# A decoder layer's attention loop: queries transposed when only centred, and a new order of the work within a step

## The chip, the cores and the metric

One core of a Trainium2 chip runs the whole layer in one launch. The metric is the device time of a run in microseconds (us). Three runs of the kernel before took 506.27, 509.51 and 511.21 us; the median is 509.51 us. The profile is one more execution, with its own time.

## The reference

x is 64 sequences of 64 tokens with 128 features; ctx_1024 has the same shape. All is float32.

```
p    = layernorm(x) @ Wv.T + bv                      # self-attention, q = k = v = p, 16 heads of 8
x    = x + softmax(p p' / sqrt(8)) p @ Wo.T + bo
q    = layernorm(x)                                  # cross-attention, no projection
x    = x + softmax(q ctx' / sqrt(8)) ctx
h    = layernorm(x)                                  # shared SwiGLU expert and one of 7 routed experts
x    = x + 0.5 / tw * shared(h) + switched(h) / tw
layernorm(x) = (x - mean) / sqrt(var + 1e-5)
```

## The kernel before, in words

**Units and steps.** A unit is 128 tokens, that is two sequences; there are 32. The first phase (`phase_a`, line 181) carries every unit through both attentions and up to the router's product. It is a software pipeline: in step t, of 38 in all, each letter of the table `DELAY` (line 177) works on the unit t minus its delay: n (first layer norm) 0, p (projections) 1, s (self-attention) 2, o (its output leaves) 3, x (residual, second layer norm, cross scores) 4, y (the weighing of cross-attention) 5, r (third layer norm, router) 6. So up to seven units are in work at once. Phases for the shared expert and the routed experts follow, from about 330 us on; the change does not touch them.

**What sets the order.** Each engine has a function `body(t, u, live)` that is written out for all steps; an engine works off its instructions strictly in the order in which `body` lists them, and waits at each for counts of semaphores. Nothing is planned at run time. A wait therefore holds up everything behind it on its engine.

**One step, by engine.** The tensor engine (PE, line 460) does: the self scores of s (L426), the transposition of the normalised tokens of p (L468), of the cross probabilities of y (L435, eight matmul records), the projections (L476, L481), the weighing of y (L447), the transposition of the normalised cross queries of x (L492), the cross scores (L426), the transposition of the self probabilities (L435), the turning back of y's output (L457), the transposition of r's tokens (L506), of o's attention output (L511), the weighing of s (L447), the router's product (L518), the output projection of o (L523), and the turning back of s (L457). Its next step begins with the self scores again. ScalarE (ACT, line 640) copies transposed tiles out of PSUM and takes the exponentials (L613); late in a step it does `exp("x", .., 0)`, then the eviction `oT_s` (L626), then `exp("x", .., 1)`. VectorE (DVE, line 797) does moments (`moments`, `mean_variance`), the residual sum (L807), the maxima of each score row and their subtraction (L769, L776) and the reciprocals and products that normalise the outputs (L784, L792). GpSimd (POOL, line 329) turns mean and variance into normalised tiles: four small instructions for the second layer norm (L334 to L342), the same for the first and third together, then the bias sum (L366), the masked keys `k_s` (L371) and y's residual sum (L376). In the code `xn["s"]` is the normalised tile of the second norm, `ps_oT`, `ps_wo` and `ps_qT` are one and the same quarter of a PSUM bank.

**The way through memory.** The self-attention output `on_s` of o is written to DRAM by head and read back by token (`orow`). The sync engine's queue (SP, line 259) issues it: two writes, four loads of cross keys, then after the writes have landed the read of `orow`, two loads of cross values, four more of keys, and a prefill. The read of `orow` is issued and waited for in the same step (L511).

These lines order the projection before:

```
if live("o"):                                         # PE, end of step t, unit t - 3
    pe.wait_ge(sem("s_onT"), at(u["o"]))
    nc.tensor.matmul(ps_wo, onT[:], wo_sb[:], start=True, stop=True).then_inc(sem("s_wo"), 1)
if live("x"):                                         # DVE, start of step t + 1, the same unit
    dve.wait_ge(sem("s_wo"), at(u["x"]))
```

Of the kernel before, what the change touches and what calls it, by code (L numbers as in the profile page):

```python
# [27 lines left out]
DK = D // H  # L28
# [29 lines left out]
def build(nc, x, ctxk, ctxv, wv, bv, wo, bo, rw, rb, wup, wdn, ident, hmask, tri, small, tokens, out):  # L58
    ctx = ExitStack()
    with ctx:  # L60
# [242 lines left out]
        def _(pool):  # L303
# [25 lines left out]
            def body(t, u, live):  # L329
                i = t % 2  # L330
                pool.wait_ge(sem("mv_set"), 2)
                if live("x"):
                    pool.wait_ge(sem("s_mv"), at(u["x"]))
                    nc.gpsimd.tensor_scalar(ve[:, 0:1], mv[i][:, 0:1, 1], EPS, None, ALU.add).then_inc(sem("s_ve"), 1)  # L334
                    if u["x"] >= 2:
                        pool.wait_ge(sem("s_xn"), u["x"] - 1)
                    pool.wait_ge(sem("s_ve"), at(u["x"]))
                    nc.gpsimd.tensor_tensor(rs[i][:, 0:1], ve[:, 0:1], mhalf[:, 0:1], ALU.pow).then_inc(sem("s_rs"), 1)
                    nc.gpsimd.tensor_scalar(nmean[i][:, 0:1], mv[i][:, 0:1, 0], -1.0, None, ALU.mult).then_inc(sem("s_mean"), 1)
                    pool.wait_ge(sem("s_rs"), at(u["x"]))  # L340
                    pool.wait_ge(sem("s_mean"), at(u["x"]))
                    normed("s", t, u["x"], xn["s"][:], "s_qT")  # L342
# [19 lines left out]
                if live("o"):  # L362
                    if u["o"] == 0:
                        pool.wait_ge(sem("obias"), 1)
                    pool.wait_ge(sem("p_xn"), at(u["o"]))
                    nc.gpsimd.tensor_tensor(x_all[:, u["o"], :], x_all[:, u["o"], :], obias[:], ALU.add).then_inc(sem("p_xb"), 1)  # L366
                if live("p"):
# [49 lines left out]
        def _(pe):  # L417
# [42 lines left out]
            def body(t, u, live):  # L460
                if live("s"):
                    pe.wait_ge(sem("s_khd"), at(u["s"]))
                    scores("s", u["s"], pT, k_s)
                if live("p"):
# [4 lines left out]
                if live("y"):  # L469
                    turn("x", u["y"], 0)  # L470
                    turn("x", u["y"], 1)
                if live("p"):
# [34 lines left out]
                if live("o"):  # L507
                    pe.wait_ge(sem(f"w_rows{u['o'] % 2}"), 16 * (u["o"] // 2 + 1))
                    if u["o"] >= 1:
                        pe.wait_ge(sem("x_q"), u["o"])  # L510
                    nc.tensor.transpose(ps_oT, orow[u["o"] % 2][:], id_sb[:]).then_inc(sem("s_oT"), 1)  # L511
# [7 lines left out]
                if live("o"):  # L519
                    if u["o"] == 0:  # L520
                        pe.wait_ge(sem("obias"), 1)
                    pe.wait_ge(sem("s_onT"), at(u["o"]))
                    nc.tensor.matmul(ps_wo, onT[:], wo_sb[:], start=True, stop=True).then_inc(sem("s_wo"), 1)  # L523
# [81 lines left out]
        def _(act):  # L605
# [5 lines left out]
            def exp(k, u, g):  # L611
# [28 lines left out]
            def body(t, u, live):  # L640
                weights_of_step(t)
                if live("p"):
# [8 lines left out]
                if live("s"):  # L651
                    exp("s", u["s"], 0)
                if live("x"):
                    act.wait_ge(sem("s_qT"), at(u["x"]))
                    if u["x"] >= 1:
                        act.wait_ge(sem("x_sc"), u["x"])
                    nc.scalar.copy(qT[:], ps_qT).then_inc(sem("x_q"), 1)  # L657
# [7 lines left out]
                if live("s"):  # L665
                    exp("s", u["s"], 1)
# [16 lines left out]
                if live("o"):  # L683
                    act.wait_ge(sem("s_oT"), at(u["o"]))
                    if u["o"] >= 1:
                        act.wait_ge(sem("s_wo"), u["o"])
                    nc.scalar.copy(onT[:], ps_oT).then_inc(sem("s_onT"), 1)
                if live("x"):
                    exp("x", u["x"], 0)
                if live("s"):  # L690
                    evicted("s", u["s"])
                if live("x"):
                    exp("x", u["x"], 1)
# [42 lines left out]
        def _(dve):  # L736
# [15 lines left out]
            def mean_variance(k, t, u):  # L752
                dve.wait_ge(sem(f"{k}_st"), at(u))
                dve.wait_ge(sem("mv_set"), 2)
                if k == "s" and u >= 2:
                    dve.wait_ge(sem("s_ve"), u - 1)
                    dve.wait_ge(sem("s_mean"), u - 1)
# [3 lines left out]
                nc.vector.bn_aggr(mv[t % 2][:, NORM[k], :], st[k][:]).then_inc(sem(f"{k}_mv"), 1)  # L761

# [34 lines left out]
            def body(t, u, live):  # L797
                if live("n"):
                    if u["n"] in X_LOADS:
                        dve.wait_ge(sem(X_LOADS[u["n"]]), 16)  # L800
                    moments("p", u["n"])
                if live("n"):
                    mean_variance("p", t, u["n"])
                if live("x"):
# [3 lines left out]
                if live("o"):  # L808
                    invert("s", u["o"])
                if live("x"):  # L810
# [221 lines left out]
```

## Time and profile before

| | |
|---|---|
| median of three runs | 509.51 us (506.27 to 511.21) |
| profiled execution | 505.83 us, its span 503.8 us |
| PE busy | 426.8 us, 85% of the span |
| PE weight loads | 321.6 us, 64% |
| DVE busy | 324.7 us, 64% |
| ACT busy | 280.8 us, 56% |
| POOL busy | 288.5 us, 57% |
| mean granted PE clock | 0.956 of full speed |

The span runs from the first to the last instruction; some 2 us of the execution lie around it. Busy shares are means over phases with different limits. PE's matmuls are pipelined, and the ends in the trace are modelled, so the distance from the start of one block to the start of the next says more than a duration. "L160" is the line of the helper that issues nearly all DMAs. Idle time named "issue" is idle with nothing in the profile to wait for.

### The profile page before, as it was taken

The page shows a single profiled execution, that of the slowest core. Times are in us where ns is not written, and L with a number is a line of the kernel's source. Part 1 is how long each engine was busy: PE and PEld are TensorE (multiplying, and loading weights), DVE is VectorE, ACT ScalarE, POOL GpSimd, SP SyncE. Part 2 cuts the span into 40 slices and gives each one's busy share as a digit, 9 for nine tenths or more (in the row PEclk, how much of TensorE's full clock was granted, in tenths as well). Part 3 has the DMA queues.
Part 4 walks back from the last instruction along what each step waited for, and adds up shares of the span by engine and source line. Part 5 has one row for each costly group of instructions (what it writes and reads, how often), then busy time and mean ns, then how long its engine had stood idle before and what let it go on. Part 6 is the DMA issues. An engine that isn't in the chain of part 4 may idle for free. (4 is left out here: it accounts for less than half of the span.)

```text
span 503.8 us, 16733 instructions
## 1 busy us (share of the span) xinstructions
PE 426.8 (85%) x5528; PEld 321.6 (64%) x5529; DVE 324.7 (64%) x959; ACT 280.8 (56%) x695; POOL 288.5 (57%) x493
## 2 busy tenths in 40 slices
PE   1688799888898988999898987588999759999991
PEld 0345456555555655555555555378999759999990
DVE  5547688875876878787887875366555514444441
ACT  2237677675676776777767664322222226666660
POOL 6867577675576676767767663404544503444443
PEclk9999999997998999999999997779999959999997
DMA  4223533544444545533332333001112134540000
GB/s 107 57 36 46 94 54 47 92 83 77 81 70 69 110 73 88 93 46 52 45 53 40 54 38 69 2 0 54 63 63 73 64 105 128 135 127 27 29 31 6
DMA packets 171647, 32.55 MB, mean 65 GB/s; under 512 B 147507, under 2 KB 169014, under 8 KB 171584
## 3 DMA queue, kind: packets, MB, share of 16 engines
q1 hardware_dynamic: 161696, 19.50, 24.6%
q10 hardware_dynamic: 7136, 5.90, 4.3%
q0 software_dynamic: 2752, 6.33, 3.6%
q8 instruction: 36, 0.59, 0.5%
q14 instruction: 27, 0.22, 0.2%
HBM read 18.26 MB, written 13.83 MB: 64 GB/s over the span
## 5 line engine op out<-in xcount | busy, mean ns | idle before, releaser
L853 DVE TENSOR_TENSOR gT<-gT,bank 128x384 f32<-128x384 f32 x70 | 38.7, 554 | 68.1 <-PE bank L542 58.7
L769 DVE TENSOR_REDUCE mx_x<-bank 128x8 f32<-128x512 f32 x64 | 41.2, 686 | 45.4 <-PE bank L426 45.4
L406 POOL DMA_INDIRECT out<-yrow,token x38 | 37.3, 982 | 55.0 <-DVE yrow L967 43.4
L701 ACT ACTIVATE gT<-bank 128x384 f32<-128x384 f32 x70 | 34.1, 487 | 53.0 <-PE bank L542 51.4
L371 POOL TENSOR_TENSOR k_s<-pT,hmask_sb 128x1024 f32<-128x1024 f32 x32 | 60.9, 1902 | 3.5 <-ACT pT L664 3.5
L551 PE MATMUL bank<-wdn_sb,gT 128*128 (+1 forms) x420 | 58.7, 276 | 2.9 <-DVE rowb L863 2.3
L542 PE MATMUL bank<-fhT,wtile 128*128 128x128 f32 x456 | 59.7, 283 | 0.0
L397 POOL DMA_INDIRECT sorted_rows<-rowb,place x32 | 31.0, 967 | 44.7 <-DVE rowb L863 28.7
L542 PEld LDWEIGHTS bank<-fhT,wtile 128*128 128x128 f32 x456 | 56.4, 199 | 0.3 <-issue 0.3
L551 PEld LDWEIGHTS bank<-wdn_sb,gT 128*128 128x128 f32 x420 | 52.7, 192 | 3.8 <-DVE gT L853 2.7
L542 PE MATMUL bank<-hT_all,wup_sb 128*128 (+1 forms) x384 | 49.4, 280 | 0.0
L769 DVE TENSOR_REDUCE mx_s<-bank 128x8 f32<-128x512 f32 x64 | 43.6, 681 | 5.4 <-PE bank L426 5.4
L542 PEld LDWEIGHTS bank<-hT_all,wup_sb 128*128 128x128 f32 x384 | 46.8, 197 | 0.0
L776 DVE TENSOR_TENSOR pr_s<-bank,mx_s 128x512 f32<-128x512 f32 x64 | 44.3, 692 | 2.2
L435 PEld LDWEIGHTS bank<-id_sb,pr_s 128*128 128x128 f32 x256 | 28.6, 146 | 26.8 <-ACT pr_s L613 26.8
L426 PE MATMUL bank<-ring,qT 64*64 64x512 f32 x256 | 35.2, 619 | 12.2 <-ACT qT L657 9.4
L613 ACT ACTIVATE pr_s<-pr_s 128x512 f32<-128x512 f32 x64 | 40.6, 635 | 3.8 <-DVE pr_s L776 3.7
L613 ACT ACTIVATE pr_x<-pr_x 128x512 f32<-128x512 f32 x64 | 40.5, 635 | 1.3 <-DVE pr_x L776 1.2
L647 ACT COPY xnT<-bank 128x128 f32<-128x128 f32 x32 | 8.5, 265 | 58.4 <-PE bank L468 58.4
L776 DVE TENSOR_TENSOR pr_x<-bank,mx_x 128x512 f32<-128x512 f32 x64 | 40.9, 681 | 0.0
L620 ACT COPY prT_s<-bank 128x512 f32<-128x512 f32 x64 | 34.6, 589 | 10.1 <-PE bank L435 10.0
L620 ACT COPY prT_x<-bank 128x512 f32<-128x512 f32 x64 | 34.8, 589 | 9.2 <-PE bank L435 9.0
(136 smaller groups left out, 917.1 us busy)
## 6 DMA issues: line engine op xcount, KB each, us to landing
sorted_rows<-nowhere_row SPq DMA_DIRECT2D x38, 129.0 KB, 2.9
ring<-sorted_rows SPq DMA_DIRECT2D x38, 129.0 KB
ring<-in_ctxk SPq DMA_DIRECT2D x256, 8.0 KB
wup_sb<-in_wup ACTq DMA_DIRECT2D x8, 352.0 KB, 3.7
ring<-in_ctxv SPq DMA_DIRECT2D x64, 32.0 KB, 3.3
attention_out<-on_s SPq DMA_DIRECT2D x64, 32.0 KB
orow<-attention_out SPq DMA_DIRECT2D x32, 64.0 KB, 1.8
x_all<-in_x ACTq DMA_DIRECT2D x3, 512.0 KB, 5.0
```

Of the source, the lines that this page charges most:

```text
L371: nc.gpsimd.tensor_tensor(k_s[:], pT[:].rearrange("p (b k) -> p b k", b=NB).unsqueeze(2).broadcast_to([P, NB, HG, S]), hmask_sb[:, 0:HG].u ...
L397: pool.indirect_dma_start(out=hs_dram, out_offset=bass.IndirectOffsetOnAxis(ap=place[p][:, 0:1], axis=0), in_=rowb[p][:, :], in_offset=Non ...
L406: pool.indirect_dma_start(out=out, out_offset=bass.IndirectOffsetOnAxis(ap=token[p][:, 0:1], axis=0), in_=yrow[p][:, :], in_offset=None, b ...
L426: last = nc.tensor.matmul(ps_s[k][g][S * b:S * (b + 1), :], q[S * g:S * (g + 1), S * b:S * (b + 1)], keys[S * g:S * (g + 1), b, :, :].rear ...
L542: last = nc.tensor.matmul(ps[p][:, c * P:(c + 1) * P], weights[:, start:start + P], tokens, start=True, stop=True)
L551: last = nc.tensor.matmul(ps_y[p], gT[p][:, c, :], wdn_sb[:, expert, c, :], start=(c == 0), stop=(c == CH - 1))
L613: nc.scalar.activation(pr[k][:, g, :, :], pr[k][:, g, :, :], ACT.Exp, scale=float(DK) ** -0.5).then_inc(sem(f"{k}_exp"), 1)
L620: nc.scalar.copy(prT[k][:, g, :, :].rearrange("p i q -> p (i q)"), ps_s[k][g][:, :]).then_inc(sem(f"{k}_prT"), 1)
L701: nc.scalar.activation(gT[p][:].rearrange("p c q -> p (c q)"), ps_gate[p][:, 0:CH * P], ACT.Silu).then_inc(sem("f_act"), 1)
L769: nc.vector.tensor_reduce(mx[k][:, g, :], scores_of(k, g), AX.X, ALU.max).then_inc(sem(f"{k}_mx"), 1)
L776: nc.vector.tensor_tensor(pr[k][:, g, :, :], scores_of(k, g), mx[k][:, g, :].unsqueeze(2).broadcast_to([P, HG, S]), ALU.subtract).then_inc ...
L853: nc.vector.tensor_tensor(g, g, ps_up[p][:, 0:CH * P], ALU.mult).then_inc(sem("f_g"), 1)
```

## The change

Five edits, all in the attention steps. The delays, the number of steps and the DMA queue's program stay as they are.

1. The second layer norm is split. VectorE subtracts the mean (`centred`), and that tile is transposed and used as the cross queries. The scores are then too large by the token's standard deviation; GpSimd computes `(8 (var + eps)) ** -0.5` and the cross exponentials take it as their per-token scale. GpSimd loses two instructions of this norm (the negated mean, the 128x128 normalisation).
2. Transposition and product of the output projection (PE), and the copy between them (ACT), move from the end of o's step to the start of the next: the transposition behind the self scores, the product behind the transposition of y's probabilities.
3. PE: half 0 of the self probabilities is transposed ahead of the cross scores, half 1 behind the turning back of y.
4. ACT: the second self exponential moves behind the eviction of half 0; the bias copy `pT` goes ahead of the copy `qT`.
5. DVE: the normalisation of o and the moments of r and n open the step; the first self half follows; then residual sum, moments and centring of x; the second self half; then y's reciprocal and product; the cross maxima and subtractions come last. Before, y's pair came last.

```diff
@@ GpSimd @@
-                if live("x"):
-                    pool.wait_ge(sem("s_mv"), at(u["x"]))
-                    nc.gpsimd.tensor_scalar(ve[:, 0:1], mv[i][:, 0:1, 1], EPS, None, ALU.add).then_inc(sem("s_ve"), 1)
...
-                    nc.gpsimd.tensor_scalar(nmean[i][:, 0:1], mv[i][:, 0:1, 0], -1.0, None, ALU.mult).then_inc(sem("s_mean"), 1)
...
-                    normed("s", t, u["x"], xn["s"][:], "s_qT")
...
+                if live("x"):
+                    pool.wait_ge(sem("s_mv"), at(u["x"]))
+                    nc.gpsimd.tensor_scalar(ve[:, 0:1], mv[i][:, 0:1, 1], EPS, float(DK), ALU.add, ALU.mult).then_inc(sem("s_ve"), 1)
+                    if u["x"] >= 2:
+                        pool.wait_ge(sem("x_exp"), G * (u["x"] - 1))
+                    pool.wait_ge(sem("s_ve"), at(u["x"]))
+                    nc.gpsimd.tensor_tensor(rs[i][:, 0:1], ve[:, 0:1], mhalf[:, 0:1], ALU.pow).then_inc(sem("s_rs"), 1)
@@ PE @@
                     scores("s", u["s"], pT, k_s)
+                if live("x"):
+                    pe.wait_ge(sem(f"w_rows{u['x'] % 2}"), 16 * (u["x"] // 2 + 1))
...
+                    nc.tensor.transpose(ps_oT, orow[u["x"] % 2][:], id_sb[:]).then_inc(sem("s_oT"), 1)
...
                     turn("x", u["y"], 1)
+                if live("x"):
+                    pe.wait_ge(sem("s_onT"), at(u["x"]))
+                    nc.tensor.matmul(ps_wo, onT[:], wo_sb[:], start=True, stop=True).then_inc(sem("s_wo"), 1)
...
                     nc.tensor.transpose(ps_qT, xn["s"][:], id_sb[:]).then_inc(sem("s_qT"), 1)
+                if live("s"):
+                    turn("s", u["s"], 0)
...
                     scores("x", u["x"], qT, kx[:, u["x"] % RING, :, :, :])
-                if live("s"):
-                    turn("s", u["s"], 0)
-                    turn("s", u["s"], 1)
                 if live("y"):
                     turn_back("x", u["y"])
+                if live("s"):
+                    turn("s", u["s"], 1)
...
-                if live("o"):
...
@@ ACT @@
                 act.wait_ge(sem(f"{k}_sub"), G * u + g + 1)
+                if k == "x":
+                    act.wait_ge(sem("s_rs"), at(u))
                 nc.scalar.activation(pr[k][:, g, :, :], pr[k][:, g, :, :], ACT.Exp,
-                                     scale=float(DK) ** -0.5).then_inc(sem(f"{k}_exp"), 1)
+                                     scale=rs[t % 2][:, 0:1] if k == "x" else float(DK) ** -0.5).then_inc(sem(f"{k}_exp"), 1)
...
+                if live("x"):
+                    act.wait_ge(sem("s_oT"), at(u["x"]))
...
+                    nc.scalar.copy(onT[:], ps_oT).then_inc(sem("s_onT"), 1)
...
                     turned("s", u["s"], 0)
+                    exp("s", t, u["s"], 1)
                     turned("s", u["s"], 1)
...
@@ DVE @@
+            def centred(t, u):
+
+                dve.wait_ge(sem("s_mv"), at(u))
+                if u >= 1:
+                    dve.wait_ge(sem("s_qT"), u)
+                nc.vector.tensor_scalar(xn["s"][:], x_all[:, u, :], mv[t % 2][:, 0, 0:1], None, ALU.subtract).then_inc(sem("s_xn"), 1)
...
+                if live("o"):
+                    invert("s", u["o"])
+                    normalise("s", u["o"])
+                if live("r"):
+                    dve.wait_ge(sem("x_x"), at(u["r"]))
+                    moments("x", u["r"])
                 if live("n"):
...
                     moments("p", u["n"])
+                if live("r"):
+                    mean_variance("x", t, u["r"])
                 if live("n"):
                     mean_variance("p", t, u["n"])
+                if live("s"):
+                    maximum("s", u["s"], 0)
+                    soften("s", u["s"], 0)
                 if live("x"):
...
+                    centred(t, u["x"])
                 if live("s"):
-                    maximum("s", u["s"], 0)
-                    soften("s", u["s"], 0)
                     maximum("s", u["s"], 1)
                     soften("s", u["s"], 1)
+                if live("y"):
+                    invert("x", u["y"])
+                    normalise("x", u["y"])
                 if live("x"):
                     maximum("x", u["x"], 0)
                     maximum("x", u["x"], 1)
                     soften("x", u["x"], 0)
                     soften("x", u["x"], 1)
-                if live("y"):
-                    invert("x", u["y"])
-                    normalise("x", u["y"])
```

## Rows read from the trace of the kernel before

**Rows 1.** Transpositions of one unit's cross queries: count, durations ns min/median/max, first and last start.

```profile
L492 PE MATMUL bank<-id_sb,xn_s x32: 327/328/329, 37.4 to 316.4; 128*128 128x128 f32 x32
```

**Rows 2.** Busy time by stretch: us, PE, PEld, DVE, ACT, POOL, clock, DMA share, GB/s.

```profile
37.44:316.42 278.98, 246.58 (x3956) 156.28 (x3952) 216.96 (x570) 194.24 (x510) 188.36 (x364) 0.97 0.42 67
72.08:80.50 8.42, 7.92 (x136) 5.08 (x132) 7.04 (x20) 6.36 (x17) 6.29 (x12) 1.00 0.36 50
```

**Rows 3.** Waits, whole span: us in total, times, longest.

```profile
PE bank L511 <- DMA orow<-attention_out: 17.1, 20, 2.9
```

**Rows 4.** Timeline, one step without a stall: start, us, instruction [idle before it].

```profile
71.06 1.09 PE L426 MATMUL bank<-k_s,pT 64*64 64x512 f32 x8
...
74.38 0.33 PE L492 MATMUL bank<-id_sb,xn_s 128*128 128x128 f32 x1
...
75.11 1.09 PE L426 MATMUL bank<-ring,qT 64*64 64x512 f32 x8 [0.40 <-issue]
...
76.12 1.09 PE L435 MATMUL bank<-id_sb,pr_s 128*128 128x128 f32 x8
...
76.25 1.29 DVE L769 TENSOR_REDUCE mx_x<-bank 128x8 f32<-128x512 f32 x2 [1.21 <-PE bank L426]
...
77.05 0.38 PE L457 MATMUL bank<-id_sb,oT_x 128*128 128x128 f32 x2
...
77.46 1.28 DVE L776 TENSOR_TENSOR pr_x<-bank,mx_x 128x512 f32<-128x512 f32 x2
...
78.17 0.63 ACT L613 ACTIVATE pr_x<-pr_x 128x512 f32<-128x512 f32 x1
...
78.65 0.25 DVE L784 RECIPROCAL rden_x<-bank 128x16 f32<-128x16 f32 x1
...
78.71 0.35 ACT L626 COPY oT_s<-bank 128x256 f32<-128x256 f32 x1
...
78.94 0.29 DVE L792 TENSOR_TENSOR on_x<-bank,rden_x 128x128 f32<-128x128 f32 x1
...
79.12 0.44 PE L457 MATMUL bank<-id_sb,oT_s 128*128 128x128 f32 x2
...
79.14 0.28 DVE L750 BATCH_NORM_STATS2 st_p<-x_all 128x6 f32<-128x128 f32 x1
...
79.48 1.09 PE L426 MATMUL bank<-k_s,pT 64*64 64x512 f32 x8
```

**Rows 5.** Timeline of the same step: other instructions that the change moves or adds to.

```profile
71.50 0.25 DVE L750 BATCH_NORM_STATS2 st_s<-x_all 128x6 f32<-128x128 f32 x1
...
71.85 0.17 DVE L761 BATCH_NORM_AGGREGATE mv<-st_s 128x2 f32<-128x6 f32 x1
...
73.03 0.69 DVE L776 TENSOR_TENSOR pr_s<-bank,mx_s 128x512 f32<-128x512 f32 x1
...
73.63 0.68 DVE L769 TENSOR_REDUCE mx_s<-bank 128x8 f32<-128x512 f32 x1
...
76.36 0.46 POOL L366 TENSOR_TENSOR x_all<-x_all,obias 128x128 f32<-128x128 f32 x1
...
78.55 0.47 PE L523 MATMUL bank<-wo_sb,onT 128*128 128x128 f32 x2
...
79.46 0.18 DVE L761 BATCH_NORM_AGGREGATE mv<-st_p 128x2 f32<-128x6 f32 x1
...
79.57 0.29 DVE L807 TENSOR_TENSOR x_all<-bank,x_all 128x128 f32<-128x128 f32 x1
```

**Rows 6.** Timeline behind attention: a copy of 128x128 within SBUF.

```profile
341.33 0.22 DVE L859 COPY rowb<-h_all 128x128 f32<-128x128 f32 x1
```

**Rows 7.** Busy time by stretch, around a stall of PE.

```profile
109.80:113.20 3.40, 2.33 (x19) 1.28 (x18) 2.36 (x4) 2.49 (x8) 3.19 (x5) 1.00 0.14 30
113.20:116.60 3.40, 2.31 (x37) 1.92 (x38) 0.96 (x5) 1.55 (x4) 0.45 (x1) 0.66 0.41 41
```

**Rows 8.** Timeline: the matmul that ended this stall.

```profile
114.29 0.47 PE L511 MATMUL bank<-id_sb,orow 128*128 128x128 f32 x1 [2.16 <-DMA orow<-attention_out]
```

More of the change, by code:

```diff
@@ L463, in body @@
                     scores("s", u["s"], pT, k_s)
+                if live("x"):
+                    pe.wait_ge(sem(f"w_rows{u['x'] % 2}"), 16 * (u["x"] // 2 + 1))
+                    if u["x"] == 0:
+                        pe.wait_ge(sem("obias"), 1)
+                    if u["x"] >= 1:
+                        pe.wait_ge(sem("x_q"), u["x"])
+                    nc.tensor.transpose(ps_oT, orow[u["x"] % 2][:], id_sb[:]).then_inc(sem("s_oT"), 1)
                 if live("p"):
@@ L506, in body @@
                     nc.tensor.transpose(ps_hT, h_all[:, u["r"], :], id_sb[:]).then_inc(sem("r_hT"), 1)
-                if live("o"):
[L508 to L511, printed above, removed]
                 if live("s"):
@@ L518, in body @@
                     nc.tensor.matmul(ps_r[:, u["r"], :], hT_all[:, u["r"], :], rw_sb[:], start=True, stop=True).then_inc(sem("r_r"), 1)
[L519 to L523, printed above, removed]
                 if live("s"):
@@ L609, in _, with exp @@
             act.wait_ge(sem("v_ones"), 4)
-            def exp(k, u, g):
+            def exp(k, t, u, g):
                 act.wait_ge(sem(f"{k}_sub"), G * u + g + 1)
+                if k == "x":
+                    act.wait_ge(sem("s_rs"), at(u))
                 nc.scalar.activation(pr[k][:, g, :, :], pr[k][:, g, :, :], ACT.Exp,
-                                     scale=float(DK) ** -0.5).then_inc(sem(f"{k}_exp"), 1)
+                                     scale=rs[t % 2][:, 0:1] if k == "x" else float(DK) ** -0.5).then_inc(sem(f"{k}_exp"), 1)
             def turned(k, u, g):
@@ L641, in body @@
                 weights_of_step(t)
+                if live("x"):
+                    act.wait_ge(sem("s_oT"), at(u["x"]))
+                    if u["x"] >= 1:
+                        act.wait_ge(sem("s_wo"), u["x"])
+                    nc.scalar.copy(onT[:], ps_oT).then_inc(sem("s_onT"), 1)
                 if live("p"):
@@ L651, in body @@
                 if live("s"):
[L652 to L657, printed above, removed]
+                    exp("s", t, u["s"], 0)
                 if live("p"):
@@ L664, in body @@
                     nc.scalar.activation(pT[:], ps_pT, ACT.Identity, bias=bv_sb[:, 0:1]).then_inc(sem("p_pT"), 1)
-                if live("s"):
-                    exp("s", u["s"], 1)
+                if live("x"):
+                    act.wait_ge(sem("s_qT"), at(u["x"]))
+                    if u["x"] >= 1:
+                        act.wait_ge(sem("x_sc"), u["x"])
+                    nc.scalar.copy(qT[:], ps_qT).then_inc(sem("x_q"), 1)
                 if live("y"):
@@ L682, in body @@
                     nc.scalar.copy(hT_all[:, u["r"], :], ps_hT).then_inc(sem("r_hTall"), 1)
[L683 to L687, printed above, removed]
                 if live("x"):
-                    exp("x", u["x"], 0)
+                    exp("x", t, u["x"], 0)
                 if live("s"):
@@ L692, in body @@
                 if live("x"):
-                    exp("x", u["x"], 1)
+                    exp("x", t, u["x"], 1)
             phase_a(body)
@@ L756, in mean_variance @@
                     dve.wait_ge(sem("s_ve"), u - 1)
-                    dve.wait_ge(sem("s_mean"), u - 1)
                 if k != "s" and t >= 2:
@@ L807, in body @@
                     nc.vector.tensor_tensor(x_all[:, u["x"], :], ps_wo, x_all[:, u["x"], :], ALU.add).then_inc(sem("s_x"), 1)
-                if live("o"):
-                    invert("s", u["o"])
-                if live("x"):
                     dve.wait_ge(sem("s_x"), at(u["x"]))
                     moments("s", u["x"])
-                if live("o"):
-                    normalise("s", u["o"])
-                if live("x"):
                     mean_variance("s", t, u["x"])
-                if live("r"):
-                    dve.wait_ge(sem("x_x"), at(u["r"]))
-                    moments("x", u["r"])
-                    mean_variance("x", t, u["r"])
+                    centred(t, u["x"])
                 if live("s"):
-                    maximum("s", u["s"], 0)
-                    soften("s", u["s"], 0)
                     maximum("s", u["s"], 1)
                     soften("s", u["s"], 1)
+                if live("y"):
+                    invert("x", u["y"])
+                    normalise("x", u["y"])
                 if live("x"):
```

6 lines of the change are left out of this document (removed).

## The prediction

> **What bounds the kernel now.** I read the busy shares first: PE is at the top, but the mean covers phases with other limits, so I cut the attention phase out. One instruction comes once a unit, the transposition of the cross queries; its first and last start give the length of a step: 279.0 us over 31 steps, 9.00 us each [rows 1, 2]. A step without a stall takes 8.42 us [rows 2]. So 31 x 0.58 = 18.0 us of this phase are disturbance. Second I read the waits: PE waited 17.1 us for the read of `orow` alone, in 20 of the 32 steps [rows 3]. That is nearly all of the 18.0, and it is what the change aims at.
>
> Third I ask what sets the 8.42 us, since a new order can change it. PE is busy 7.92 us of them and DVE 7.04 [rows 2], neither all of it, so a chain through several engines closes on itself. I follow it in the timeline of one step [rows 4], from one self score block (71.06) to the next (79.48):
> - PE works in order from the self scores to the transposition of the queries: 74.38 - 71.06 = 3.32.
> - Its end, ACT's copy, the cross scores: 75.11 - 74.38 = 0.73.
> - Cross scores until DVE can begin: 76.25 - 75.11 = 1.14. DVE had sat idle 1.21 before it, so it is not the limit here.
> - Two maxima 1.21 (to 77.46), the first subtraction 0.71 (to 78.17), then ACT's exponential of half 0.
> - The eviction `oT_s` stands behind that exponential in ACT's order: 0.54 (to 78.71). PE's turning back of s waits for it: 0.41 (to 79.12). The next self scores stand behind that: 0.36 (to 79.48). The row at 79.12 shows PE idle for this eviction.
>
> 3.32 + 0.73 + 1.14 + 1.21 + 0.71 + 0.54 + 0.41 + 0.36 = 8.42, the whole step. What lengthens this chain costs its full length in every step.
>
> **The change part by part.**
>
> *The wait for `orow`.* From `on_s` to `orow` the way through DRAM has now one step more. The longest wait was 2.9 us [rows 3] and a step is over 8, so it is gone, and with it the stretch at low clock that followed a stall [rows 7, 8]. I give back all 18.0 us. SP's program is the same, its queue has as much work per step, and `on_s` is ready as early in a step as before. Late next is no DMA but the chain.
>
> *The projection ahead of the queries.* The transposition of `orow` and the product stood where PE waited anyway for `oT_s`. Now both lie in the first piece of the chain. Eight records of a transposition block take 77.05 - 76.12 = 0.93 from start to start, 0.116 each [rows 4]; one for the transposition and two for the product make 0.35. Bounds: 0 if they fit into a hole; 0.80 if each cost its duration (the product 0.47 [rows 5], a transposition 0.33 as at 74.38 [rows 4]). I take 0.35, for the block is back to back work of the same form. The copy between the two is now first in ACT's order; PE is at y's transpositions meanwhile, so it costs nothing. Without that cover it would be one such copy, under 0.35 (the larger one at 78.71).
>
> *Centring on DVE, and the wait for it.* After the self scores start (time 0), PE reaches the product at 1.01 (self scores, as 75.11 to 76.12) + 0.12 + 0.12 + 0.93 = 2.18 and it ends at 2.65. DVE: the turning back of s ends at 0.08 (79.12 + 0.44 against 79.48); reciprocal and product 0.49 (78.65 to 79.14) [rows 4]; moments of two norms twice 0.43 (79.14 to 79.57); a maximum 0.72 and a subtraction 0.60 (73.03 to 73.63) [rows 5]. That adds up to 2.79 with one handoff of 0.04 (78.65 + 0.25 to 78.94), so it and PE's product come nearly together. Then, each with 0.04 for the handoff: residual sum 0.33, moments 0.29, aggregate 0.21, and the centred tile, for which I take the 0.22 of a copy of the same size in SBUF [rows 6]: ready at 3.88. PE would be there at 3.32 + 0.35 = 3.67. So 0.21 of waiting. Bounds: 0, if the two moments overlap fully; 0.7, if centring waits for GpSimd as in the rival below. GpSimd's two instructions that go were off the chain, and its standard deviation is due only at the cross exponentials, nearly 5 us later: no gain, no loss.
>
> *Half 0 of the self transpositions between queries and cross scores.* It takes 0.47 of the 0.62 in which PE waited for ACT's copy. On the chain nothing changes: 0.73 stays. Half 1 moves behind the turning back and waits for an exponential that ACT now does later; its followers (weighing, router) are due only at the turning back of s. From y's turning back to there the new step has 3.8 us; PE's work in it is 2.07 of before (77.05 to 79.12), less 0.35, plus 0.47 for the half: 2.2. The 1.6 left cover a late exponential of 0.63, so I cost it at 0; without that cover it would be those 0.63.
>
> *The turning back of y and y's reciprocal ahead of the cross maxima.* This is the dear part. DVE now may not begin the cross maxima when the scores are there. It first waits for the turning back, which PE issues behind the cross scores, and then does y's pair. Instead of 1.14: cross scores 1.01, turning back 0.38, handoff 0.04, makes 1.43; then the pair, 0.49 [rows 4]. That is 0.78 more. The second self half ends on DVE at 3.84 + 0.72 + 0.69 = 5.25, the turning back of y at 3.88 + 0.73 + 1.39 = 6.00, so DVE stands idle between and nothing fills it. Bounds: 0.29 if the pair were free, 0.83 with both durations in full.
>
> *The tail of the chain* is as before, 3.23: the eviction `oT_s` still stands behind the first cross exponential.
>
> Sum: 3.32 + 0.35 + 0.21 + 0.73 + 1.43 + 0.49 + 3.23 = 9.76 us a step, 1.34 more than an undisturbed one and 0.76 more than today's mean. It applies to the steps in which x, y and s are all live, t = 5 to 33, 29 of them: 38.9 us. In the others the chain has no eviction of s; I count them as even. From the profiled execution: 505.83 - 18.0 + 38.9 = 526.7 us.
>
> **The clock.** In today's stalled step PE was busy 2.33 of 3.40 us, and after it the granted clock fell to the lower of its levels, 1.2 GHz in place of 2.4, for part of the next stretch (a mean of 0.66) [rows 7]. The wait before that matmul was 2.16 us [rows 8]. The new step leaves PE 1.6 us idle in its second half (above), in two or more pieces. The undisturbed steps, with 0.5 us idle, show no fall. I put two falls of some 3.4 us into the forecast, each costing half of that: 3.4 us. Forecast 530 us. The execution profiled lies 3.7 us below the median; I correct nothing for that, since runs likely differ by the very stalls that go. A measurement here can tell about 1% from no change.
>
> **Rivals.**
> - *The clock falls in every third step* (0.20). For it: the idle pieces come back in all 29 steps. Against it: none is as long as the 2.16 us. Ten falls at 1.7 us are 17, at twice that 34: 544 to 561 us.
> - *Centring meets GpSimd* (0.20). About when DVE centres, GpSimd does, by the order of its program, the last of its normalisations or the bias sum, 0.46 us [rows 5]; if one must wait for the other's instruction, the query transposition comes up to 0.46 later: 29 x 0.46 = 13.3 us, 543 us. No row here has DVE do a one-input operation within SBUF beside a busy GpSimd, so the trace says nothing against it. The Trainium skill, SBUF — State Buffer, section Who interferes with whom, states that a `tensor_scalar` from SBUF to SBUF can take the port pair that DVE shares with GpSimd, and that the later of the two is fully blocked; by that rule this rival is the forecast.
> - *The chain does not bind, an engine does* (0.08, the other side: faster). If the two added waits of DVE and the eviction found slack that I overlooked, a step would cost what the busiest engine needs: PE 7.92, DVE 7.04 plus 0.22 and its handoffs, some 8.2. Then 505.83 - 18.0 - 29 x 0.2 = 482 us. It decides where DVE reaches the cross maxima no later than 0.1 us after the cross scores end. Against it: the eight terms fill the step of today without a remainder, and two added ones stand in DVE's own order. [...]
> - *Half of the lengthening is hidden* (0.06): the step is 9.0 to 9.1 and the two sides cancel, 505 to 508 us.
> - *The wait for `orow` stays* (0.03), because SP is late with the writes: then 17 us return, 547.
>
> **The numbers.** My forecast has 0.43, the rivals 0.57 together. The range is 516 to 552. Below, the unknown costs at their low ends (no wait for centring, -6; half of the 0.35, -5; no falls, -3). Above, the port and the clock rivals, without the worst of the latter. Outside are the faster case, the even one and part of the clock's. Slower by over 1%: 0.43 + 0.20 + 0.20 + 0.03 = 0.86; within 1%: 0.06; faster: 0.08.
>
> **What the new profile would show.** Steps of 9.7 to 9.9 us by the starts of the query transpositions. No wait of PE for `orow`. DVE idle before y's reciprocal, about 0.9 us in each step, where it was idle before the cross maxima; ACT idle before the first cross exponential; PE idle about 1 us before the turning back of s, released by `oT_s`. The query transposition 3.9 us behind the self scores: 4.3 would be the port. The forecast is wrong if steps come out below 9.2, or if the mean clock of the phase falls below 0.9.

## The result, and the profile after

The new kernel takes 574.01 us (median of 4 runs, 565.32 to 579.82) against 507.89 before (median of 4): 1.122 times as long, 95% interval 1.101 to 1.142. Each ratio, here and below, compares the fast runs alone (of the new kernel those of 565.32 and 573.71 us), so it is not the quotient of the two medians. The execution that was profiled is the longest of the four, 579.82 us, with the lowest mean clock: 0.863 of full speed, where the four have 0.914, 0.895, 0.892 and 0.863 in order of their time. What is counted in it below is therefore the worst of the four. I had forecast 530 with a range up to 552. The direction and the new wait are as forecast; the size is not.

The page of the new kernel (busy us, share, instructions; then PE's granted clock in tenths over 40 slices):

```profile
PE 469.1 (81%) x5528; PEld 346.1 (60%) x5529; DVE 347.9 (60%) x991; ACT 294.1 (51%) x695; POOL 266.2 (46%) x429
...
PEclk9858778787978978877887989977899996999997
```

PE is busy 42 us more for the same work, and the clock line is full of sevens and eights, where only a few slices of the kernel before fall below nine tenths. The transpositions of the cross queries, once a unit, give the step again, as in [rows 1]:

```profile
L498 PE MATMUL bank<-id_sb,xn_s x32: 327/328/473, 40.6 to 389.2; 128*128 128x128 f32 x32
```

348.6 us over 31 steps, 11.25 each, where it was 9.00. Three stretches of one step each show what the mean is made of; the first row is the whole phase (columns as in [rows 2]):

```profile
40.63:389.24 348.61, 288.12 (x3951) 180.14 (x3952) 237.76 (x600) 206.60 (x509) 166.09 (x301) 0.84 0.33 53
192.78:203.00 10.22, 7.97 (x132) 4.98 (x133) 8.05 (x21) 6.72 (x17) 5.52 (x11) 1.00 0.45 76
203.00:215.38 12.38, 10.77 (x132) 6.76 (x132) 7.89 (x21) 6.86 (x17) 5.75 (x11) 0.72 0.38 69
215.38:226.88 11.50, 9.60 (x140) 5.99 (x132) 7.75 (x21) 6.97 (x18) 5.60 (x10) 0.85 0.39 67
```

At the full clock, 2.4 GHz, a step takes 10.22 us. Where the clock was at its lower level, 1.2 GHz, for part of the step (mean 0.72 or 0.85), the same instructions take 12.38 or 11.50. In 22 of the 31 steps the mean is below 1: 20 inside the loop, of 11.3 to 12.4 us, and the last two, 9.99 and 9.07, in which little work is left. In the kernel before it was 3. So two things happened: the step at full clock grew from 8.42 to 10.22 us, and the clock fell again and again. The waits name the place of the first:

```profile
PE bank L453 <- ACT oT_s L625: 33.2, 32, 1.6
...
DVE rden_x L788 <- PE bank L453: 35.7, 32, 3.6
```

Of the waits for `orow`, 17.1 us in [rows 3], a single one of 0.7 us is left. PE waits for `oT_s` in all 32 steps. The timeline of one step at full clock has the chain of [rows 4], with the new links:

```profile
182.18 0.29 DVE L765 TENSOR_SCALAR xn_s<-x_all,mv 128x128 f32<-128x128 f32 x1
...
182.53 0.33 PE L498 MATMUL bank<-id_sb,xn_s 128*128 128x128 f32 x1 [0.29 <-DVE xn_s L765]
...
183.26 1.09 PE L422 MATMUL bank<-ring,qT 64*64 64x512 f32 x8
...
184.28 0.44 PE L453 MATMUL bank<-id_sb,oT_x 128*128 128x128 f32 x2
...
184.75 0.26 DVE L788 RECIPROCAL rden_x<-bank 128x16 f32<-128x16 f32 x1 [0.96 <-PE bank L453]
...
185.25 1.28 DVE L773 TENSOR_REDUCE mx_x<-bank 128x8 f32<-128x512 f32 x2
...
186.45 1.28 DVE L780 TENSOR_TENSOR pr_x<-bank,mx_x 128x512 f32<-128x512 f32 x2
...
187.16 0.72 ACT L612 ACTIVATE pr_x<-pr_x,rs 128x512 f32<-128x512 f32 x1 [0.67 <-DVE pr_x L780]
...
187.79 0.35 ACT L625 COPY oT_s<-bank 128x256 f32<-128x256 f32 x1
...
188.20 0.44 PE L453 MATMUL bank<-id_sb,oT_s 128*128 128x128 f32 x2 [1.07 <-ACT oT_s L625]
...
188.56 1.09 PE L422 MATMUL bank<-k_s,pT 64*64 64x512 f32 x8
...
190.73 0.39 PE L477 MATMUL bank<-wo_sb,onT 128*128 128x128 f32 x2
...
191.22 0.29 DVE L822 TENSOR_TENSOR x_all<-bank,x_all 128x128 f32<-128x128 f32 x1
...
191.77 0.45 POOL L326 TENSOR_SCALAR xn_p<-x_all,nmean,rs 128x128 f32<-128x128 f32 x1
...
192.10 0.63 DVE L765 TENSOR_SCALAR xn_s<-x_all,mv 128x128 f32<-128x128 f32 x1
...
192.19 0.46 POOL L355 TENSOR_TENSOR x_all<-x_all,obias 128x128 f32<-128x128 f32 x1
...
192.78 0.33 PE L498 MATMUL bank<-id_sb,xn_s 128*128 128x128 f32 x1 [0.64 <-DVE xn_s L765]
```

Query transposition to cross scores 0.73; these to y's reciprocal, behind the turning back, 1.49; the pair 0.50; two maxima 1.20; first subtraction 0.71; scaled exponential 0.63 from start to start; `oT_s` 0.41; turning back of s to the self scores 0.36; from there to the next query transposition 4.22. Sum 10.25, the length of this step.

The second thing, a fall of the clock, looks like this in the step of 12.38 us. The clock is still at its upper level when the step begins at 203.00, and goes down some 5 us later, beside PE's wait for `oT_s`:

```profile
208.20:214.60 6.40, 5.97 (x42) 3.77 (x46) 3.01 (x10) 3.07 (x8) 2.44 (x6) 0.50 0.41 82
```

```profile
208.63 0.69 PE L453 MATMUL bank<-id_sb,oT_s 128*128 128x128 f32 x2 [1.03 <-ACT oT_s L625]
```

In all it stays down for 6.8 us in this step, and for 3.4 us in the step of 11.50.

### The profile page after: what moved, and what is told of

It reads as the page before. It is cut to its first block and busy times, and to the rows that moved or that the text cites. A ratio compares the mean times of both kernels' runs of the same rounds, so it can differ in the third digit from the quotient of the medians.

```text
span 577.5 us, 16708 instructions
## 1 busy us (share of the span) xinstructions
PE 469.1 (81%) x5528; PEld 346.1 (60%) x5529; DVE 347.9 (60%) x991; ACT 294.1 (51%) x695; POOL 266.2 (46%) x429
## 5 line engine op out<-in xcount | busy, mean ns | idle before, releaser
L337 POOL TENSOR_SCALAR ve<-mv 128x2 f32<-128x2 f32 x38 | 8.8, 231 | 141.2 <-DVE mv L758 140.9
L612 ACT ACTIVATE pr_x<-pr_x,rs 128x512 f32<-128x512 f32 x64 | 46.0, 721 | 23.9 <-DVE pr_x L780 23.9
L431 PE MATMUL bank<-id_sb,pr_x 128*128 128x128 f32 x256 | 51.1, 366 | 3.7 <-ACT pr_x L612 3.7
L422 PE MATMUL bank<-k_s,pT 64*64 64x512 f32 x256 | 52.8, 908 | 0.0
L431 PE MATMUL bank<-id_sb,pr_s 128*128 128x128 f32 x256 | 41.9, 288 | 13.2 <-ACT pr_s L612 13.2
L619 ACT COPY prT_s<-bank 128x512 f32<-128x512 f32 x64 | 37.5, 586 | 26.6 <-PE bank L431 25.9
L539 PE MATMUL bank<-hT_all,wup_sb 128*128 (+1 forms) x384 | 50.6, 284 | 0.0
L431 PEld LDWEIGHTS bank<-id_sb,pr_x 128*128 128x128 f32 x256 | 46.1, 199 | 4.2 <-ACT pr_x L612 4.2
L619 ACT COPY prT_x<-bank 128x512 f32<-128x512 f32 x64 | 36.5, 587 | 18.2 <-PE bank L431 17.1
L453 PE MATMUL bank<-id_sb,oT_s 128*128 128x128 f32 x64 | 17.3, 360 | 33.2 <-ACT oT_s L625 33.2
```

Source lines behind the costliest of these rows:

```text
L422: last = nc.tensor.matmul(ps_s[k][g][S * b:S * (b + 1), :], q[S * g:S * (g + 1), S * b:S * (b + 1)], keys[S * g:S * (g + 1), b, :, :].rear ...
L431: last = nc.tensor.transpose(ps_s[k][g][:, i * P:(i + 1) * P], pr[k][:, g, 2 * i:2 * i + 2, :].rearrange("p h k -> p (h k)"), id_sb[:])
L539: last = nc.tensor.matmul(ps[p][:, c * P:(c + 1) * P], weights[:, start:start + P], tokens, start=True, stop=True)
L619: nc.scalar.copy(prT[k][:, g, :, :].rearrange("p i q -> p (i q)"), ps_s[k][g][:, :]).then_inc(sem(f"{k}_prT"), 1)
```

## Experiments on the new kernel

The kernel before, run on the same chip beside each group, took 506.6 to 508.2 us; each ratio is to it.

**e1, the holes filled.** Two transpositions ahead of half 1, and these eight ahead of the turning back of s:

```
+                if live("s") and live("x"):
+                    for _ in range(8):
+                        nc.tensor.transpose(bank[7][:, P:2 * P], id_sb[:], id_sb[:])
```

> The new kernel with ten transpositions added on PE in each step, two ahead of self half 1 and eight ahead of the turning back of s, where PE waits; their results go to an unused part of a PSUM bank and nobody reads them. Chain and clock theory: the steps without a fall take 10.22 us because of the chain, and the 11.50 and 12.38 us of the others come from PE's low clock behind idle time. With the holes filled the clock holds, nearly all steps take 10.2 to 10.4 us, and the time falls by about 31 x 1.0 = 30 us, to 540 to 550. Rival, the clock is not moved by this idle time (or the long steps are long for another reason): no change in the mix of steps, 574 us or more, for the fillers only add work.

Measured: 544.0 us, ratio 1.076 (1.068 to 1.084). The phase and two steps:

```profile
37.80:345.11 307.31, 276.25 (x4252) 180.94 (x4252) 237.70 (x600) 203.00 (x508) 164.52 (x301) 1.00 0.38 60
147.89:157.91 10.02, 9.12 (x143) 5.99 (x143) 7.85 (x21) 6.73 (x17) 5.46 (x11) 1.00 0.45 77
157.91:168.17 10.26, 9.15 (x142) 6.01 (x143) 8.04 (x21) 6.74 (x17) 5.81 (x12) 1.00 0.45 77
```

Ten more instructions on PE in every step, and the kernel is 30 us faster by the medians, 23 by the two ratios. The whole phase ran at full clock but for its last step; it took 307.3 us instead of 348.6. So the idle time let the clock fall, and that cost 23 to 30 us, and 41 in the profiled execution, the worst of the four. What is left, 9.91 us a step, is the chain. It comes in two lengths in the main, 9.88 and some 10.2, which the next run explains.

**e2, GpSimd's bias sum first.** The block of L355 moved to the front of GpSimd's `body`.

> The new kernel with GpSimd's bias sum moved from behind its normalisations to the front of its step, where it waits over 4 us anyway; GpSimd's following work is then done 0.46 us earlier. Port theory: centring took 0.63 us beside a busy GpSimd and 0.29 beside an idle one; now it takes 0.29 to 0.35 everywhere and a step at full clock 9.85 to 9.95 instead of 10.22, about 10 us less in all if the clock falls as often. Rival, the 0.63 has nothing to do with GpSimd: step at full clock 10.22, no change. Either way falls of the clock stay.

Measured: 560.0 us, ratio 1.105 (1.096 to 1.114). The phase, a step with a fall, one without:

```profile
37.83:370.88 333.05, 273.26 (x3951) 169.71 (x3951) 235.29 (x600) 204.74 (x508) 164.98 (x301) 0.89 0.34 56
176.50:188.05 11.55, 9.65 (x141) 5.99 (x133) 7.75 (x21) 6.96 (x18) 5.58 (x10) 0.85 0.36 62
188.05:197.93 9.88, 7.97 (x133) 4.99 (x133) 7.72 (x21) 6.71 (x17) 5.50 (x10) 1.00 0.44 78
```

Now all 13 complete steps at full clock take 9.87 to 9.92 us (10.22 came before), and centring takes 0.28 to 0.32 us in all 32 steps, where 6 took 0.63 in the new kernel. The total is 14 us below the new kernel by the medians, 9 by the ratios; 17 steps still have a fall. In the timeline above the slow one (192.10) begins while GpSimd's normalisation (191.77 to 192.22) runs, the fast one (182.18) follows a pause of GpSimd. The port rival of the prediction was a real effect of 0.34 us, but only in steps at full clock where the two meet: 6 of 32 in the new kernel, 12 in e1, 24 in e3 and in e4 below. By the rule of the Trainium skill, SBUF — State Buffer, section Who interferes with whom, the later one is blocked until the other ends; the trace agrees if the bias sum is counted too. Of the normalisation only 0.12 us was left, but the bias sum follows it at once (192.19 to 192.65), and the slow centring ends 0.08 behind it, at 192.73. So do all the delayed ones of the new kernel, e1, e3, e4 and e10, 96 in number: each ends 0.07 to 0.10 us behind the end of a GpSimd instruction. In e10 that is the normalisation, and centring mostly takes 0.35 to 0.36. Who is later is a close matter: in e1 a centring that also begins 0.32 behind the start of the normalisation (76.91) takes 0.29 us, and then the bias sum is the longer one, 0.50 instead of 0.45.

**e3, y's pair late again.**

```
                 if live("x"):
                     maximum("x", u["x"], 0)
...
+                if live("y"):
+                    invert("x", u["y"])
+                    normalise("x", u["y"])
```

> The new kernel with y's reciprocal and product behind the cross maxima and subtractions on DVE again, as in the kernel before; nothing else changed. Chain theory: the wait for the turning back and the pair, 1.50 + 0.50, become about 1.14 in the chain, a step at full clock 9.4 to 9.5 instead of 10.22; PE is idle 0.8 us less, so falls get rarer too: 535 to 550 us. Rival, the order on DVE has slack and the loss is the clock's alone: step at full clock stays 10.2, total within 5 us of 574.

Measured: 519.0 us, ratio 1.026 (1.019 to 1.033). Cross scores and maxima, then a step:

```profile
153.94 1.09 PE L422 MATMUL bank<-ring,qT 64*64 64x512 f32 x8
...
155.09 1.29 DVE L773 TENSOR_REDUCE mx_x<-bank 128x8 f32<-128x512 f32 x2 [0.61 <-PE bank L422]
```

```profile
153.21:162.69 9.48, 8.00 (x132) 5.02 (x132) 8.04 (x21) 6.62 (x17) 5.84 (x12) 1.00 0.47 83
```

The maxima start 1.15 us behind the scores, as before the change (1.14), and the step takes 9.48: 0.74 less, the term of 0.78. The total fell by 55 us by the medians, 48 by the ratios, far more than 31 x 0.74 = 23. The rest is the clock: 2 steps with a fall, the first and the last of the phase, instead of 22. My expectation of 535 to 550 missed that the falls would end at once.

**e4, the eviction first.** In ACT's `body`, `evicted("s", ..)` stands ahead of `exp("x", .., 0)`.

> The new kernel with ACT's eviction of the self output ahead of the first cross exponential instead of behind it. Chain theory: the chain of the step goes through that eviction; released from the exponential, PE turns s back and starts the next step about 1 us earlier, and another chain through DVE takes over, 9.2 us a step at full clock instead of 10.22; fewer falls, 525 to 545 us. Rival, the wait before the turning back is only where idle time collects and DVE's own order sets the step: step at full clock stays 10.2, the idle time shows up elsewhere, 574 us.

Measured: 521.0 us, ratio 1.026 (1.017 to 1.034). The eviction, the exponential, the turning back, then a step:

```profile
158.13 0.37 ACT L625 COPY oT_s<-bank 128x256 f32<-128x256 f32 x1 [0.38 <-PE bank L443]
...
158.50 0.72 ACT L612 ACTIVATE pr_x<-pr_x,rs 128x512 f32<-128x512 f32 x1
...
158.55 0.44 PE L453 MATMUL bank<-id_sb,oT_s 128*128 128x128 f32 x2 [0.17 <-ACT oT_s L625]
```

```profile
153.78:163.13 9.35, 8.04 (x132) 4.99 (x132) 8.00 (x21) 6.82 (x17) 5.80 (x12) 1.00 0.44 84
```

The turning back no longer waits for the exponential. 9.35 us a step: one exchange of two neighbours on ACT gives 53 us by the medians, 49 by the ratios, and the total is 4 us under the range that I expected. The next chain, through DVE, is as long as expected within 0.15; in the steps inside the loop PE's longest wait in total is now that for the centred tile, 15.4 us in 25 steps.

**e9, both and the bias sum.**

> The new kernel with three moves together: y's pair behind the cross work on DVE again, ACT's eviction ahead of the first cross exponential, GpSimd's bias sum at the front. Everything else of the change stays (centring, projection early in the next step, the split self transpositions). Chain theory: both parts of the chain that made it long are gone, the next chain (self half through DVE, centring, second self half) gives about 8.9 us a step, no falls of the clock, no wait for the attention output: 279 - 31 x 0.1 in the phase, in all about 500 to 505 us, level with the kernel before. Rival, the gains of the single moves add up (10.22 - 0.74 - 0.86 - 0.34 = 8.3): 485.

```profile
132.79:141.81 9.02, 7.98 (x132) 4.99 (x132) 7.70 (x21) 6.71 (x17) 5.49 (x11) 1.00 0.39 62
```

Measured: 507.6 us, ratio 1.000 (0.996 to 1.004). That is 3 us over the range that I expected. The single gains do not add up. e3 and e4 both still have the slow centring in 24 steps; without its 0.34 us e4's 9.35 would be 9.01, the step of e9. So once the eviction is early, the place of y's pair is worth nothing more, and once y's pair is late (9.48, less 0.34 is 9.14), the eviction is worth 0.1. What is left of the change is worth nothing against the kernel before: it traded 18 us of waiting for `orow` for 31 steps that are 0.6 us longer each.

**e10, the projection late again.** The new kernel with a stage w of delay 4 between o and x, in which the transposition of `orow` stands behind that of r's tokens and the product behind the router's, as in the kernel before; x, y and r one step later.

> The new kernel without edit 2's place: transposition and product of the projection again late in a step, one step after the output left (stage w, x, y and r a step later). My prediction's terms: 0.35 for PE's two blocks and 0.21 for DVE's wait leave the chain, 10.22 to about 9.7 us at full clock. Chain theory with DVE's own order: the centred tile comes when DVE has worked through the opening of its step, about 3.6 to 3.9 us behind the self scores, whatever PE does; the gain is 0.1 to 0.2 only, 10.0 to 10.1 us a step. Falls of the clock as before in both; 560 to 575 us.

Measured: 542.8 us, ratio 1.066 (1.060 to 1.072).

```profile
149.67:159.46 9.79, 8.21 (x132) 4.99 (x133) 7.67 (x21) 6.72 (x17) 5.47 (x11) 1.00 0.45 78
```

The total is 17 us under the 560 to 575 that I expected, because the falls did not stay: 4 steps have one, the first and the last three of the phase, and none inside the loop. The step is 9.79 us, nearer to the 9.7 of my two terms than to the 10.0 to 10.1 that I set against them. Against the 9.88 of e2, in which centring is undelayed too, the place of the projection is worth 0.09 us; the rest of the way from 10.22 is that DVE centres earlier and hardly meets GpSimd (0.35 us for the tile in most steps). So of the 0.56 us that I charged, the place of PE's two blocks was the small part; DVE's own order was the large one.

## Experiments on the kernel before

**e5, the projection one step later, at its old place.** The edit on PE; ACT's is alike:

```
-    DELAY = {"n": 0, "p": 1, "s": 2, "o": 3, "x": 4, "y": 5, "r": 6}
+    DELAY = {"n": 0, "p": 1, "s": 2, "o": 3, "w": 4, "x": 5, "y": 6, "r": 7}
-                if live("o"):
+                if live("w"):
-                    pe.wait_ge(sem(f"w_rows{u['o'] % 2}"), 16 * (u["o"] // 2 + 1))
+                    pe.wait_ge(sem(f"w_rows{u['w'] % 2}"), 16 * (u["w"] // 2 + 1))
```

> The kernel before with only the aim of edit 2, put where the chain does not see it: projection at the same place at the end of a step, but one step after the unit's output left (a stage w between o and x; x, y and r one step later, one step more in all). Chain theory: no wait for the read of the attention output, undisturbed steps stay at 8.4 us, the 18 us of disturbance go and one step of 8.4 us comes: about 497 us, 2% under the kernel before. Rival, the waits come from the transfers as such and find another place (keys, values): then 506 to 515 us.

```profile
46.49:307.80 261.31, 240.45 (x3876) 152.03 (x3877) 209.75 (x562) 191.32 (x501) 185.58 (x361) 0.98 0.43 70
130.74:139.12 8.38, 7.92 (x139) 5.05 (x132) 7.03 (x20) 6.37 (x18) 6.28 (x13) 1.00 0.58 95
```

Measured: 494.6 us, ratio 0.980 (0.974 to 0.987). The 18 us of the prediction are real: 8.43 us a step instead of 9.00, and one step more. The aim of edit 2 was right; its place on PE was not needed for it.

**e6, the eviction first, on the kernel before.** The exchange of e4.

> The kernel before with ACT's eviction of the self output ahead of the first cross exponential, nothing else. Chain theory: an undisturbed step gets shorter by the wait PE had there, 8.42 to about 8.1 us; if the waits for the attention output keep their size, 31 x 0.3 = 9 us less, about 497. Rival, a shorter step only makes PE wait longer for the read of the attention output, whose way is a fixed time: the steps in which it waits stay as long as they are and the total falls by under 4 us.

```profile
PE bank L511 <- DMA orow<-attention_out: 19.2, 19, 3.0
```

Measured: 507.6 us, ratio 1.008 (1.003 to 1.014). The rival holds: the undisturbed step falls to 8.18 us as expected, and PE waits 19.2 us for `orow` instead of 17.1, with 9.01 us a step in the mean. A shorter step only meets the transfer earlier.

**e7, centring alone.** Edit 1 on the kernel before, GpSimd's scale behind its bias sum.

> The kernel before with edit 1 alone: DVE centres directly behind the aggregate of the second norm, GpSimd makes only the scale, behind its bias sum; the order of everything else is that of before. Chain theory: GpSimd's normalisation was off the chain, so nothing is won; the cross exponential with a per-token scale takes 0.72 instead of 0.63 us and lies in the chain, an undisturbed step is 8.5 instead of 8.42, in all 0 to 4 us more, 507 to 511. Rival, the earlier queries shorten the step: below 8.3 us and 500 or less.

```profile
140.93:149.40 8.47, 8.00 (x139) 5.04 (x133) 7.15 (x21) 6.43 (x18) 5.23 (x10) 1.00 0.52 89
```

Measured: 509.4 us, ratio 1.003 (0.997 to 1.010). 8.47 us where most undisturbed steps of the kernel before take 8.38 and some 8.42: the per-token scale on the exponential (0.72 us against 0.63) is in the chain, and nothing is won.

**e8, e5 and e6 together.**

> Both at once, the later projection and the earlier eviction, on the kernel before. Chain theory: steps of 8.1 us without waits, 506.6 - 18 - 9 + 8 = about 487 us, the best of all so far. Rival, SP or another chain binds next at 8.4: 497 as with the later projection alone.

```profile
43.38:301.61 258.23, 239.22 (x3884) 152.82 (x3877) 209.91 (x562) 196.52 (x501) 185.43 (x361) 0.97 0.43 70
127.02:135.20 8.18, 7.83 (x132) 5.05 (x132) 7.06 (x20) 6.68 (x18) 6.28 (x12) 1.00 0.55 95
```

Measured: 490.6 us, ratio 0.971 (0.964 to 0.979). 8.18 us a step; with the transfer out of the way the exchange pays. The mean is 8.33, so some 5 us of single delays stay, and the total is 4 us over the expectation.

**e11, and the place that centring makes possible.** On e8, with edit 1:

```
+                if live("x"):
+                    pe.wait_ge(sem("s_xn"), at(u["x"]))
+                    nc.tensor.transpose(ps_qT, xn["s"][:], id_sb[:]).then_inc(sem("s_qT"), 1)
                 if live("y"):
                     pe.wait_ge(sem(f"l_vx{u['y'] % RING}"), V_UNIT * (u["y"] // RING + 1))
```

> The kernel before with the later projection and the earlier eviction (487 to 492 so far), plus edit 1, and the place that edit 1 makes possible: the transposition of the centred queries ahead of the weighing of y, ACT's copy ahead of the first self exponential, so that the copy is hidden by the weighing and the cross scores follow without a hole. Chain theory: the 0.6 us hole in front of the cross scores goes, the scaled exponential is off the chain; about 7.9 us a step instead of 8.18, 31 x 0.25 = 8 us less, about 483 us. Rival, ACT or DVE is the bound near 8.2: 490.

Query transposition, weighing, ACT's copy, cross scores; then the phase and a step:

```profile
155.79 0.33 PE L484 MATMUL bank<-id_sb,xn_s 128*128 128x128 f32 x1
...
156.04 0.65 PE L443 MATMUL bank<-prT_x,ring 128*32 128x64 f32 x32
...
156.15 0.27 ACT L653 COPY qT<-bank 128x128 f32<-128x128 f32 x1 [0.20 <-PE bank L484]
...
156.63 1.09 PE L422 MATMUL bank<-ring,qT 64*64 64x512 f32 x8
```

```profile
42.49:290.29 247.80, 239.26 (x3851) 151.49 (x3845) 221.19 (x592) 199.69 (x500) 159.78 (x295) 0.99 0.45 74
147.84:155.79 7.95, 7.85 (x140) 5.11 (x133) 7.16 (x21) 6.72 (x18) 5.23 (x11) 1.00 0.55 97
```

Measured: 486.0 us, ratio 0.955 (0.950 to 0.960), the fastest of all. The weighing covers the copy: 0.59 us from its start to the cross scores, and PE waits for nothing there. The plain step takes 7.95, others up to 8.5; what those wait for I did not take apart.

**e12, y's pair first, on e5.**

> The kernel before with the later projection (495 us, steps of 8.38) and edit 5's dear part alone: y's reciprocal and product ahead of the cross maxima on DVE. Chain theory: at least 0.78 more a step by the term of the prediction, 9.2 us; and as in this order DVE finishes its step later, the second norm behind it (moments, GpSimd's four instructions, queries) becomes part of the chain too, up to 10.1 us. With over 1.5 us of PE idle the clock begins to fall: 520 to 560 us. Rival, y's pair fits beside other work: under 8.6 us a step, 495 to 500.

```profile
148.35:159.98 11.63, 9.47 (x137) 5.85 (x133) 7.22 (x19) 6.40 (x17) 5.58 (x11) 0.85 0.33 56
159.98:170.06 10.08, 7.92 (x138) 5.05 (x133) 6.47 (x18) 6.42 (x18) 4.64 (x9) 1.00 0.42 75
```

Measured: 555.1 us, ratio 1.090 (1.084 to 1.096). Moving two short DVE instructions, 0.5 us together, ahead of four long ones costs 60 us against e5 by the medians, 56 by the ratios: the step at full clock goes from 8.38 to 10.08, and 9 of 31 steps have a fall. No run here shows the 1.5 us of my expectation as a limit: e10 leaves PE 1.6 us idle a step and has no fall inside the loop.

## Why the prediction was wrong, point by point

- **What bounds the kernel**: right. The chain of eight terms set the step before and, with its new links, after; e4 and e12 moved it by single exchanges as it says.
- **The wait for `orow`**: right, gone but for 0.7 us, and 18 us was its size (e5).
- **The projection ahead of the queries and the wait for centring, 0.35 + 0.21**: the sum was about right where centring goes undelayed. Self scores to query transposition measured 4.22 with the 0.34 of the collision and 3.88 in e2 without it (194.05 to 197.93); I had 3.88. The split between PE and DVE was not (e10). The centred tile took 0.29 us and not the 0.22 of the copy; PE's product and DVE's work before it came together as forecast.
- **y's pair ahead of the maxima, 0.78**: 0.74 (e3).
- **The tail of the chain "as before, 3.23"**: 3.31 in the timeline above. I had read that GpSimd's scale comes in time, which it does, and not that an exponential with a scale per token takes 0.72 us instead of 0.63. A small term, missed. The Trainium skill, ScalarE: Activation LUTs, prices it in its section What ACT_TABLE_LOAD costs: about 93 ns for each operand that is a column of 128 values. The trace agrees, 0.09 us.
- **GpSimd and centring**: a rival at 0.20 that took place, at 0.34 us where I had up to 0.46, and in 6 of 32 steps here, not in all 29. In the total it is small: 2 us here, 4 in e1.
- **The clock**: this is the step that failed. "I put two falls of some 3.4 us into the forecast" was sized by the kernel before, where the clock falls behind a rare stall. The new order has its 2 us of idle in every step. Measured: falls in 22 of 31 steps of the profiled execution, 41 us there, and 23 to 30 us by the runs of e1, against the 3.4 of the sum. The price of one was about right, and the number was wrong: the 20 inside the loop cost 1.1 to 2.2 us each over 10.22, 1.7 in the mean, as I had taken. That was partly luck, for 3.4 us is the width of the stretch that I had cut out in [rows 7], and the fall there lasts twice as long (the row below this list). My own sign of being wrong came: the mean clock of the phase is 0.84, under 0.9. I had seen the idle time, even given a rival to it, but at ten steps and 0.20, on the ground that no single piece is as long as 2.16 us. It needed no such piece: PE's wait for `oT_s`, the longest that comes back in every step, was never over 1.6 us.

The fall of the kernel before, behind the wait of [rows 8]:

```profile
114.20:121.00 6.80, 6.71 (x56) 4.36 (x56) 2.99 (x11) 2.40 (x6) 2.34 (x8) 0.51 0.67 122
```

Put together: 526.7 by the chain; the profiled execution of e1, the chain without falls, took 537.7, 11.0 more, of which 7.4 lies between the first and the last query transposition (307.3 us, 299.9 by my sum: 279.0 - 18.0 + 38.9) and the rest outside them. Of the 7.4, the slow centring is 12 x 0.34 = 4.1 and the scaled exponential 29 x 0.08 = 2.3. The falls make it 574 in the median run.

## What to carry to other kernels

In engines that work in a fixed order, find the chain that closes on itself from one step to the next and check its terms against the length of a step. Then ask of every moved instruction what it now stands in front of: two short DVE instructions and one eviction decided 48 to 60 us each time here, while PE's and DVE's busy time in a step at full clock hardly changed (7.97 and 8.05 us in the new kernel, 8.04 and 8.00 in e4). And if a new order gives PE a hole in every step, price the clock in every step, not as the rare event that it was.

## What the runs showed of the hardware

- Useless transpositions in the holes of a loop made it 23 to 30 us faster, by holding PE's clock at 2.4 GHz (e1). In how many steps the clock fell, beside PE's mean idle time in the steps at full clock: e4 1.4 us, 1 of 31 steps; e3 1.5 us, 2; e10 1.6 us, 4; e2 1.95 us, 17; e12 2.1 us, 9; new kernel 2.15 us, 22. Those of e4, e3 and e10 are all in the first step or the last three of the phase. Idle time alone does not put the runs in order: why e12 had fewer than e2 stays open.
- In the new kernel a step in which the clock falls is 1.3 us longer than 10.22 where the low level lasts 3.4 us, and 2.2 us longer where it lasts 6.8. That is less than half of the low stretch, for PE has less idle time in such a step: 9.60 busy of 11.50, against 7.97 of 10.22. Behind each low stretch the clock was back at its upper level, until the next fall.
- Beside 128x128 instructions of GpSimd a DVE instruction of 0.29 us from SBUF to SBUF took up to 0.63, and ended 0.07 to 0.10 us behind the end of GpSimd's (96 cases in five runs); moving one GpSimd instruction removed it (e2).
